# A flag for integer weights found from products of their low parts on TensorE, with new head and tail tables

## What is computed

```python
x = L0_attn_x                       # 16 x 512 x 256
xn = _layernorm(x, axis=-1)
s = _L0_attn_ref(xn, Wq, Wk, Wv, Wo)          # 16 heads of 16, causal softmax, 512 x 512 scores
gate = einsum('bsd,hd->bsh', xn, w_gate / 127)    # integers -127..127, 768 hidden
up = einsum('bsd,hd->bsh', xn, w_up / 127)
g = _silu(einsum('bsh,dh->bsd', silu(gate) * up, w_down / 127))
return x + s * g
```

## Time and profile before

| | us |
|---|---|
| median of three runs | 966.6 |
| the profiled execution's own time | 964.34 |
| its span, first to last instruction | 962.6 |
| TensorE busy | 928.8 |
| VectorE busy | 704.9 |
| ScalarE busy | 585.0 |
| GpSimd busy | 492.2 |

### The profile page before, as it was taken

The page is one execution under the profiler, slowest core; times in us unless marked ns, Lnnn a source line. Parts: engine busy times, 40 slices in busy tenths (PEclk is TensorE's granted clock), DMA queues, the critical chain, the costliest instruction groups (busy, mean ns, idle before and its releaser), DMA issues.

```text
span 962.6 us, 22685 instructions
## 1 busy us (share of the span) xinstructions
PE 928.8 (96%) x9034; PEld 686.4 (71%) x9034; DVE 704.9 (73%) x950; ACT 585.0 (61%) x796; POOL 492.2 (51%) x672
## 2 busy tenths in 40 slices
...
PEclk9889999999999999999999999999999999999999
...
GB/s 251 133 68 167 80 125 137 115 177 148 125 170 124 149 124 166 148 110 174 127 157 132 149 152 108 176 107 188 128 134 160 124 168 104 180 146 124 124 80 108
DMA packets 85323, 133.97 MB, mean 139 GB/s; under 512 B 13536, under 2 KB 35808, under 8 KB 85216
## 3 DMA queue, kind: packets, MB, share of 16 engines
...
## 4 chain that ended last, share of the span: by engine, by line
PE 82%; issue 5%; DVE 4%; ACT 4%; POOL 3%; DMA 2%; SPq 0%; ACTq 0%; POOLq 0%; DVEq 0%
PE bank L193 43%; PE values L528 13%; PE bank L433 11%; PE bank L495 9%; PE bank L446 4%; ACT probs L503 2%; POOL o_compact L569 2%; DVE row_max L458 1%; DVE gated L378 1%; ACT o_hi L576 1%; PE bank L464 1%; DVE low_parts L668 1%; POOL probs L510 1%; DVE xt_lo L278 0%; DMA o_reciprocals<-scratch_r 0%
## 5 line engine op out<-in xcount | busy, mean ns | idle before, releaser
L458 DVE TENSOR_REDUCE row_max<-bank 128x2 f32<-128x768 f32 (+3 forms) x352 | 384.4, 1124 | 70.4 <-PE bank L446 66.9
L503 ACT ACTIVATE probs<-bank 128x1024 f32<-128x1024 f32 x320 | 320.2, 1025 | 124.5 <-PE bank L495 124.3
L510 POOL TENSOR_SCALAR_AFFINE_SELECT probs<-probs 128x256 f32<-128x256 f32 (+1 forms) x448 | 192.5, 447 | 290.0 <-ACT probs L503 287.6
L528 PE MATMUL values<-probs,v 128*17 128x512 f32 (+3 forms) x2048 | 166.4, 436 | 1.0 <-POOL probs L510 0.4
L433 PE MATMUL bank<-k_stack,q_stack 64*128 64x128 f32 (+3 forms) x1024 | 159.4, 370 | 5.9 <-DVE row_max L458 2.6
L392 POOL TENSOR_TENSOR h_lo<-gated,h_hi 128x512 fp32r<-128x512 f32 x96 | 124.0, 1294 | 56.6 <-ACT h_hi L389 54.5
L495 PE MATMUL bank<-q_stack,k_stack 64*128 64x512 f32 (+3 forms) x1024 | 142.7, 352 | 5.8 <-issue 4.8
L433 PEld LDWEIGHTS bank<-k_stack,q_stack 64*128 64x128 f32 x1024 | 85.4, 187 | 74.3 <-issue 32.0
L495 PEld LDWEIGHTS bank<-q_stack,k_stack 64*128 64x128 f32 x1024 | 83.2, 186 | 46.5 <-issue 23.2
L365 DVE SCALAR_TENSOR_TENSOR gated<-gated,bank 128x512 f32<-128x512 f32 x96 | 65.8, 685 | 52.3 <-ACT gated L362 52.2
L446 PE MATMUL bank<-causal_mask,half_identities_bf 64*128 64x128 bf16 (+3 forms) x1408 | 99.7, 227 | 0.0
...
## 6 DMA issues: line engine op xcount, KB each, us to landing
...
```

Of the source, the lines that this page charges most:

```text
L458: signal(e.tensor_reduce(rows, scores, axis=AX.X, op=ALU.max), "d_sm")
L503: signal(e.activation(PR[:, (SCORES * beta + k) % SLOTS, :, :], both(banks), ACT.Exp, scale=SCALE_S), "d_ex")
L510: last = e.affine_select(out=diag, in_=diag, compare_op=ALU.is_ge, fill=0.0, base=0, pattern=[[0, many], [1, P]], channel_multiplier=-1)
L528: last = nc.tensor.matmul(PVB[32 * c:32 * c + VW, j * P:S], V[par][:, j, 4 * g + c, :], PR[:, (SCORES * beta + 5 * g + kind) % SLOTS, pari ...
```

## The change

The three reductions of low parts on VectorE go. A new unit `gm k` (k = 0, 1, 2 for g, u, d) is issued on TensorE: 12 matmuls each. Each takes a 128-column block of a low part as the stationary operand and 256 columns of the same low part, the block among them, as the moving one. All 36 add up in the same 256 columns of `values`. On the diagonal of a block stand sums of squares, so the result is zero everywhere only if the low parts are. `fl 0 0` on VectorE now waits for the last of the 36 and reduces the 128 x 256 result to a column. The rest of `fl` stays, with new semaphore counts. The first `pv` of batch 0 now waits until the flag's row has been read, since it writes the same bank.

The tables `HEAD` and `TAIL` are replaced by others of the same units (plus `gm`), in another order and with other banks. `PERIOD` is the same.

```diff
+        def u_gm(en, e, beta, par, k, banks, prev):
+            if en == "pe":
+                low = W["gud"[k]][1]
+                weights_split(e, 0, "gud"[k])
+                blocks = [(t, a) for t in range(low.shape[1]) for a in range(0, low.shape[2], P)]
+                for n, (t, a) in enumerate(blocks):
+                    b = min(a, low.shape[2] - 2 * P)
+                    last = nc.tensor.matmul(PVB[:, 0:2 * P], r(low[:, t, a:a + P]), r(low[:, t, b:b + 2 * P]),
+                                            start=k == 0 and n == 0, stop=k == 2 and n == len(blocks) - 1)
+                if k == 2:
+                    last.then_inc(s_flag, 1)
+
         def u_fl(en, e, beta, par, k, banks, prev):
             if en == "dve" and k == 0:
-                e.wait_ge(c_wl, len(W))
-                for i, w in enumerate("gud"):
-                    e.tensor_reduce(LOW[:, i:i + 1], W[w][1][:].rearrange("p t n -> p (t n)"), axis=AX.X, op=ALU.max,
-                                    apply_absolute_value=True).then_inc(s_flag, 1)
-                e.wait_ge(s_flag, 3)
-                e.tensor_reduce(LOW[:, 3:4], LOW[:, 0:3], axis=AX.X, op=ALU.max).then_inc(s_flag, 1)
+                e.wait_ge(s_flag, 1)
+                e.tensor_reduce(LOW[:], PVB[:, 0:2 * P], axis=AX.X, op=ALU.max, apply_absolute_value=True).then_inc(s_flag, 1)
```

```diff
 u_pv, on pe, k == 0:
+                    if beta == 0:
+                        e.wait_ge(s_flag, 4)
```

The part of `HEAD` up to the branch, before and after:

```diff
-    ld 1 0, la 0 0, lb 0 0, wt 0 0, tr 0 0 6, tr 0 1 1, wt 0 1, wt 0 2, qk 0 0 6, wt 0 3, qk 0 1 2, wt 0 4, gg 0 0 1, wt 0 5,
-    ls 0 0, gg 0 1 5, gu 0 0 6, ls 0 1, wt 0 6, qk 0 2 2, qk 0 3 5, sm 0 0 34, mk 0 0 34, ls 0 2, sm 0 1 01, mk 0 1 01,
-    gu 0 1 6, la 1 0, hs 0 0, sm 0 2 56, xr 0 0, mk 0 2 56, sm 0 3 23, mk 0 3 23, gg 0 2 4, lm 1 0, v 0 0 1, sm 0 4 56,
-    mk 0 4 56, sm 0 5 23, mk 0 5 23, sm 0 6 01, sm 0 7 56, mk 0 6 01, mk 0 7 56, sm 0 8 34, sm 0 9 01, mk 0 8 34, mk 0 9 01,
-    sm 0 10 34, mk 0 10 34, sm 0 11 56, fl 0 0, ls 0 3, rw 0 0, mt 0 0 2, gu 0 2 3, sm 0 12 01, mk 0 11 56, gg 0 3 4, mk 0 12 01,
-    v 0 1 2, sm 0 13 34, lt 1 0, hs 0 1, lc 1 0, mk 0 13 34, sm 0 14 56, ld 2 0, mk 0 14 56, hs 0 2, sm 0 15 01, mk 0 15 01,
-    gg 0 4 2, st 0 0 56, st 0 1 34, st 0 2 01, fl 0 1, if 0 0,
+    la 0 0, lb 0 0, wt 0 0, wt 0 1, tr 0 0 2, tr 0 1 0, wt 0 2, qk 0 0 3, wt 0 3, qk 0 1 5, gg 0 0 6, gg 0 1 4, gg 0 2 3,
+    wt 0 4, qk 0 2 6, gu 0 0 5, gu 0 1 4, sm 0 0 01, sm 0 1 34, wt 0 5, mk 0 0 01, mk 0 1 34, lt 1 0, ls 0 0, sm 0 2 56,
+    mk 0 2 56, qk 0 3 2, gm 0 0, sm 0 3 01, mk 0 3 01, hs 0 0, sm 0 4 56, sm 0 5 34, mk 0 4 56, mk 0 5 34, v 0 0 2,
+    sm 0 6 56, mk 0 6 56, ls 0 1, ls 0 2, ls 0 3, sm 0 7 34, mk 0 7 34, sm 0 8 56, sm 0 9 01, mk 0 8 56, sm 0 10 23,
+    mk 0 9 01, sm 0 11 45, mk 0 10 23, mk 0 11 45, hs 0 1, ld 1 0, gu 0 2 0, wt 0 6, mt 0 0 6, ld 2 0, gg 0 3 2, gg 0 4 4,
+    gu 0 3 3, gm 0 1, v 0 1 4, la 1 0, sm 0 12 23, sm 0 13 01, mk 0 12 23, mk 0 13 01, st 0 0 45, sm 0 14 56, st 0 1 34,
+    mk 0 14 56, gm 0 2, fl 0 0, sm 0 15 34, mk 0 15 34, st 0 2 56, st 0 3 12, fl 0 1, st 0 4 56, sm 0 16 34, mk 0 16 34,
+    pv 0 0, hs 0 2, lm 1 0, sm 0 17 01, lc 1 0, if 0 0,
```

The end of `TAIL`, before and after:

```diff
-    gu 1 3 2, st 1 13 34, st 1 14 01, pv 1 6, st 1 15 23, st 1 16 01, pv 1 7, or 1 0, st 1 17 45, pv 1 8, st 1 18 12,
-    st 1 19 34, ob 1 0, op 0 0 6, pv 1 9, pv 1 10, on 1 0, pv 1 11, od 1 1, op 0 1 1, os 1 0, gg 1 4 6, gg 1 5 3, hs 1 3,
-    or 1 1, gu 1 4 3, gu 1 5 4, hs 1 4, hs 1 5, os 1 1, ob 1 1, xr 1 0, on 1 1, zr 0 0, zr 1 0, dn 1 1 4, op 1 0 6, op 1 1 1""")
+    st 1 13 56, pv 1 6, st 1 14 12, op 0 0 0, st 1 15 56, or 1 0, st 1 16 01, zr 1 0, pv 1 7, pv 1 8, st 1 17 45, ob 1 0,
+    st 1 18 23, st 1 19 01, pv 1 9, on 1 0, hs 1 3, pv 1 10, pv 1 11, od 1 1, op 0 1 4, os 1 0, gg 1 4 4, gu 1 4 1, hs 1 4,
+    or 1 1, gg 1 5 5, ob 1 1, gu 1 5 1, xr 1 0, hs 1 5, os 1 1, dn 1 1 0, on 1 1, op 1 0 5, op 1 1 6""")
```

More of the change, by code:

```diff
@@ L59 @@
-    sm 0 10 34, mk 0 10 34, sm 0 11 56, fl 0 0, ls 0 3, rw 0 0, mt 0 0 2, gu 0 2 3, sm 0 12 01, mk 0 11 56, gg 0 3 4, mk 0 12 01,
-    v 0 1 2, sm 0 13 34, lt 1 0, hs 0 1, lc 1 0, mk 0 13 34, sm 0 14 56, ld 2 0, mk 0 14 56, hs 0 2, sm 0 15 01, mk 0 15 01,
-    gg 0 4 2, st 0 0 56, st 0 1 34, st 0 2 01, fl 0 1, if 0 0, st 0 3 56, sm 0 16 34, mk 0 16 34, gu 0 3 2, sm 0 17 01,
-    st 0 4 34, mk 0 17 01, pv 0 0, st 0 5 56, sm 0 18 01, mk 0 18 01, st 0 6 34, pv 0 1, lb 1 0, sm 0 19 56, la 2 0,
-    st 0 7 12, mk 0 19 56, dn 0 0 0, gg 0 5 3, gu 0 4 2, st 0 8 56, sm 0 20 01, sm 0 21 34, mk 0 20 01, mk 0 21 34, pv 0 2,
@@ new lines @@
+    mk 0 14 56, gm 0 2, fl 0 0, sm 0 15 34, mk 0 15 34, st 0 2 56, st 0 3 12, fl 0 1, st 0 4 56, sm 0 16 34, mk 0 16 34,
+    pv 0 0, hs 0 2, lm 1 0, sm 0 17 01, lc 1 0, if 0 0, st 0 5 56, mk 0 17 01, pv 0 1, sm 0 18 23, sm 0 19 01, st 0 6 45,
+    mk 0 18 23, lb 1 0, mk 0 19 01, dn 0 0 6, gg 0 5 2, hs 0 3, rw 0 0, gu 0 4 1, xr 0 0, sm 0 20 56, mk 0 20 56, sm 0 21 34,
+    mk 0 21 34, pv 0 2, gu 0 5 0, lx 1 0, st 0 7 56, pv 0 3, st 0 8 23, hs 0 4, mt 0 1 4, st 0 9 56, qk 1 0 1, hs 0 5,
+    qk 1 1 2, gg 1 0 4, v 1 0 6, gu 1 0 5, ls 1 0, st 0 10 12, la 2 0, gg 1 1 6, qk 1 2 5, ls 1 1, lm 2 0, gu 1 1 2,
@@ new lines @@
+    gg 1 2 4, qk 1 3 1, sm 1 0 56, sm 1 1 34, mk 1 0 56, pv 0 4, st 0 11 01, mk 1 1 34, gu 1 2 2, ls 1 2, pv 0 5, sm 1 2 01,
+    mk 1 2 01, sm 1 3 56, mk 1 3 56, st 0 12 34, sm 1 4 34, ls 1 3, mk 1 4 34, sm 1 5 01, mk 1 5 01, st 0 13 56, pv 0 6,
+    sm 1 6 23, mk 1 6 23, sm 1 7 56, mk 1 7 56, st 0 14 01, dn 0 1 4, hs 1 0, sm 1 8 01, mk 1 8 01, od 0 0, sm 1 9 56,
+    st 0 15 23, mk 1 9 56, pv 0 7, pv 0 8, sm 1 10 34, st 0 16 01, mk 1 10 34, gg 1 3 2, st 0 17 01, or 0 0, hs 1 1, lt 2 0,
+    sm 1 11 45, mk 1 11 45, pv 0 9, mt 1 0 0, st 0 18 23, sm 1 12 56, mk 1 12 56, st 0 19 01, gg 1 4 4, hs 1 2, zr 0 0,
@@ new lines @@
+    v 1 1 2, ob 0 0, sm 1 13 01, mk 1 13 01, sm 1 14 34, st 1 0 56, mk 1 14 34, lc 2 0, on 0 0, pv 0 10, pv 0 11, st 1 1 56,
+    st 1 2 23, od 0 1, sm 1 15 01, mk 1 15 01, gu 1 3 4, gu 1 4 0, lb 2 0, sm 1 16 45, os 0 0, mk 1 16 45, st 1 3 23,
+    dn 1 0 6, gg 1 5 2, gu 1 5 0, sm 1 17 34, mk 1 17 34, lx 2 0, st 1 4 56, st 1 5 12, hs 1 3, or 0 1, pv 1 0, pv 1 1,
+    sm 1 18 45, sm 1 19 01, mk 1 18 45, st 1 6 23, mk 1 19 01, qk 2 0 6, sm 1 20 45, mk 1 20 45, ob 0 1, qk 2 1 2, ls 2 0,
+    ls 2 1, pv 1 2, st 1 7 01, sm 1 21 34, hs 1 4, mk 1 21 34, gg 2 0 5, mt 1 1 6, st 1 8 34, on 0 1, pv 1 3, qk 2 2 2,
@@ new lines @@
+    os 0 1, ls 2 2, qk 2 3 0, st 1 9 56, pv 1 4, sm 2 0 23, mk 2 0 23, st 1 10 01, sm 2 1 45, mk 2 1 45, op 0 0 6, hs 1 5,
+    st 1 11 23, sm 2 2 45, mk 2 2 45, sm 2 3 01, pv 1 5, mk 2 3 01, st 1 12 23, sm 2 4 56, mk 2 4 56, gg 2 1 4, st 1 13 01,
+    sm 2 5 23, ls 2 3, mk 2 5 23, sm 2 6 56, pv 1 6, mk 2 6 56, st 1 14 34, sm 2 7 12, mk 2 7 12, pv 1 7, sm 2 8 56,
+    mk 2 8 56, st 1 15 34, op 0 1 0, sm 2 9 56, mk 2 9 56, st 1 16 23, st 1 17 01, od 1 0, pv 1 8, sm 2 10 34, mk 2 10 34,
+    sm 2 11 56, mk 2 11 56, gu 2 0 0, dn 1 1 4, hs 2 0, or 1 0, xr 1 0, mt 2 0 1, v 2 0 6, gu 2 1 2, sm 2 12 45, sm 2 13 01,
@@ L84 @@
+    mk 2 12 45, mk 2 13 01, st 1 18 23, gg 2 2 6, v 2 1 4, st 1 19 23, sm 2 14 56, hs 2 1, mk 2 14 56, pv 1 9, sm 2 15 34,
+    st 2 0 01, mk 2 15 34, pv 1 10""")
 PERIOD = table("""
@@ L98 @@
 TAIL = table("""
[L99 to L102, removed]
-    gu 1 3 2, st 1 13 34, st 1 14 01, pv 1 6, st 1 15 23, st 1 16 01, pv 1 7, or 1 0, st 1 17 45, pv 1 8, st 1 18 12,
-    st 1 19 34, ob 1 0, op 0 0 6, pv 1 9, pv 1 10, on 1 0, pv 1 11, od 1 1, op 0 1 1, os 1 0, gg 1 4 6, gg 1 5 3, hs 1 3,
-    or 1 1, gu 1 4 3, gu 1 5 4, hs 1 4, hs 1 5, os 1 1, ob 1 1, xr 1 0, on 1 1, zr 0 0, zr 1 0, dn 1 1 4, op 1 0 6, op 1 1 1""")
+    ob 0 0, sm 1 16 23, mk 1 16 23, pv 0 11, sm 1 17 56, mk 1 17 56, od 0 1, sm 1 18 01, mk 1 18 01, os 0 0, on 0 0,
+    st 1 1 34, gg 1 3 2, st 1 2 56, st 1 3 34, sm 1 19 01, mk 1 19 01, pv 1 0, gu 1 2 6, st 1 4 01, sm 1 20 23, mk 1 20 23,
+    sm 1 21 45, hs 1 2, pv 1 1, mk 1 21 45, or 0 1, st 1 5 12, gu 1 3 6, mt 1 1 0, st 1 6 34, pv 1 2, st 1 7 12, st 1 8 56,
+    st 1 9 34, on 0 1, dn 1 0 0, pv 1 3, st 1 10 56, st 1 11 12, pv 1 4, ob 0 1, pv 1 5, os 0 1, zr 0 0, st 1 12 34, od 1 0,
+    st 1 13 56, pv 1 6, st 1 14 12, op 0 0 0, st 1 15 56, or 1 0, st 1 16 01, zr 1 0, pv 1 7, pv 1 8, st 1 17 45, ob 1 0,
+    st 1 18 23, st 1 19 01, pv 1 9, on 1 0, hs 1 3, pv 1 10, pv 1 11, od 1 1, op 0 1 4, os 1 0, gg 1 4 4, gu 1 4 1, hs 1 4,
+    or 1 1, gg 1 5 5, ob 1 1, gu 1 5 1, xr 1 0, hs 1 5, os 1 1, dn 1 1 0, on 1 1, op 1 0 5, op 1 1 6""")
 BRANCH = [kind for kind, *_ in HEAD].index("if")
@@ L144, in build @@
         GATES = sb("gates", [P, 2, TT, E])
-        LOW = sb("low_parts", [P, 4])
+        LOW = sb("low_parts", [P, 1])
         LOW1 = sb("low_parts_all", [1, 1])
```

12 lines of the change are left out of this document (5 added, 7 removed).

## The result

| | before | changed |
|---|---|---|
| median, us | 966.6 | 976.4 |
| profiled execution, own time / span, us | 964.34 / 962.6 | 976.94 / 975.2 |

The ratio is 1.0099 (95% interval 1.0082 to 1.0116), 8 to 11 us more. The forecast was 965.2 with a range up to 969.5, and 0.1 for slower by over 0.5%.

A forecast was written before the change was run, and what follows sets the result against it. TensorE was taken to bound most of the span, VectorE's chain the time of the branch. Terms of -0.2, -0.5, -0.4 and -0.3 summed to -1.4 us, putting the median at 965.2, range 961.5 to 969.5.

The forecast's parts named there:

- last matmul ahead of the branch ends: End of TensorE's work ahead of the branch in the new `HEAD`, put at 56.7 us.
- from there to the first behind it: TensorE's wait at the branch: 4.3 us from flag to first matmul, with 0.5 taken as hidden.
- lost to the clock behind the branch: Behind the branch TensorE again runs in part at 1.2 GHz, losing 1.9 us as before.
- waits in the rest of `HEAD`: Behind the branch, `st`, `pv` and `mt` ahead of `qk 1 0` can win back 0.4 us of waits.
- tail: New `TAIL`: 0 to 1.1 us gained by moving `op 0 0`, 0.4 bound of loss from late `ob 1 0`; -0.3 taken.
- Moved DMAs (`rw`, `xr`, `ld 1`, `lt 1`) have consumers several us away: Rest of `HEAD`: the moved transfers are needed only several us later; no cost was put on them.
- the branch's 4.3 us: From flag to first matmul behind the branch; 4.3 us that the change does not remove.
- the walk: The new `HEAD` followed unit by unit to the branch, with 3.5 us of TensorE waits ahead of it.
- rival (b): Ahead of the branch the clock falls from about 38 us, as before: +3.3 us, 968.5; chance 0.25.
- VectorE's chain sets the time of the branch: Ahead of the branch, VectorE (busy 28.2 of 29 us) sets the time; the change relieves it of 4.8 us net.
- The branch's overlap: `pv 0 0` and `sm 0 17` (1.3 us) may hide part of the 4.3 us; bounds 0 and -1.3, -0.5 taken.

The follow-up runs named there:

- The runs: DMAs of `rw` and `xr` moved: earlier in the changed kernel, ratio 1.0067 to before; onto the branch in the kernel before, ratio 1.0050.
- The run with three products: Changed kernel with 3 of the 36 products of low parts, one per weight; 975.21 us, ratio 1.0096 to before.
- relief for VectorE alone: Kernel before with the three reductions of low parts moved from VectorE to ScalarE, nothing added to TensorE; 969.04 us, ratio 1.0010.
- in the old tables: Kernel before, its tables kept, with `gm` and the new `fl` put in; 969.4 us, ratio 1.0017.
- the two mended runs: Changed kernel with `rw` and `xr` early and the old `TAIL`: 970.72 us, ratio 1.0023; the same with 3 of 36 products: 968.32 us, 1.0006.
- the zeros last: Kernel before with the new `TAIL`, its two `zr` entries put back near the end; 968.75 us, ratio 1.0012 to before.
- early fills: Changed kernel with the DMAs of `rw` and `xr` moved up in SP's order to behind `ld 1 0`; 971.86 us, ratio 1.0067 to before.
- the quiet run: The kernel before as profiled, DMA share 0.01 from 54 to 58 us; flag to first matmul 4.28 us, own time 964.34 us.

## Why the prediction was wrong

The sum was -1.4 us, the profiled execution gave +12.6. Term by term:

| step | forecast | profile of the changed kernel | difference |
|---|---|---|---|
| last matmul ahead of the branch ends | 56.7 | 59.8 | +3.1 |
| from there to the first behind it | 3.8 | 7.1 | +3.3 |
| lost to the clock behind the branch | 1.9 | 2.6 | +0.7 |
| waits in the rest of `HEAD` | -0.4 | +1.8 | +2.2 |
| tail | -0.3 | +3.6 | +3.9 |

They add to 13.2 of the 14.0 us between -1.4 and +12.6. `PERIOD` has 0.1 of the rest, and 0.7 is not placed.

**The step that failed** is "Moved DMAs (`rw`, `xr`, `ld 1`, `lt 1`) have consumers several us away", with the branch's 4.3 us taken as fixed. It asked who waits for the transfers, and not who shares the DMA engines with them. A row of before showed that they stood at a share of 0.01 during the branch; the walk followed TensorE past the branch but not SP, which doesn't branch and issued `rw` right behind `lc 1 0` (53.87 and 54.28 us). The runs show it in both directions: 7.10 to 3.37 us, and 4.77 to 9.45. The run with three products (3.99) is the exception.

**The walk** was right. It gave 3.5 us of waits ahead of the branch; the profile has 3.5. The 3.1 us are rival (b): the clock was 0.52 to 0.50 from 38 to 44 us. Where it stayed up, in the run with the new head and the old tail, the last matmul ended at 56.32 (63.98 less 7.66), 0.4 from the forecast. The clock in this stretch differs between runs with the same head: in that one it was 1.00 from 40 to 46.

**"VectorE's chain sets the time of the branch"** was wrong. VectorE was full, but TensorE from 40.8 on was full too, and relief for VectorE alone brought nothing. From 38.47 to 53.20 us TensorE waited 0.7 us in all, and that is about the most that VectorE's relief could give. So the change had next to nothing to gain there, and its products came on top: 0.0017 (1.0007 to 1.0027) in the old tables, and 0.0017 again between the two mended runs.

**The tail.** The path was right (`zr 1 0` holds SP, with the third store and `ob 1 0` behind it, and `sums` waits for `ob 1 0`), its size was not: 0.4 us was put as the bound, and 0.0028 was measured (2.7 us). The bound counted the issue, put at 0.6 us and 0.47 in the trace. It did not count the landing, which took 1.1 us more with the zeros in flight. The rest of the tail's cost, 0.0012, was not taken apart. With the zeros last `sums` still waits for the reciprocals' chain, where before it waited for the last store to land.

**The branch's overlap.** By the Trainium skill's queue of 64 (TensorE: Matmul & The Clock Gate, "Architectural detail: the array is 16× 32×32, not 1× 128×128") the whole 1.3 us would be hidden. The two profiles with all products and early fills don't bear it out: 0.9 of the quiet run's 4.28 us was hidden in one, and nothing in the other. They don't bear out the 0.5 taken either.

**Open.** The rest of `HEAD` waits 1.8 us more, 2.0 in all for exponentials ahead of score products. No run took this order apart. When the clock falls near 38 us and when not is not settled either: it fell in three of the four profiles with this `HEAD` and all 36 products. So part of the 3.1 us is the luck of the profiled execution.
